# Layer-3 queries of batch 0 behind the last chunk's front, and a longer planned duration for ScalarE's sums

## The chip, the cores and the metric

One Trainium2 chip, one core. The metric is the device time of one execution in microseconds. An execution's profile gives its span, from the first to the last instruction.

## The reference

Two sequences of 1024 tokens with 256 features (`x`), and a context of 154 tokens for each, pass through four layers. Every layer adds a cross attention and then a feed-forward network, both on the layer-normed stream:

```python
x = x + xattn_0(layernorm(x), ctx);  x = x + ffn_0(layernorm(x))   # softmax attention; ternary weights, squared ReLU
x = x + xattn_1(layernorm(x), ctx);  x = x + ffn_1(layernorm(x))   # softmax attention; gathered experts + gated MLP
x = x + xattn_2(layernorm(x), ctx);  x = x + ffn_2(layernorm(x))   # attention with rotary positions; 8 experts, top 2, + shared
x = x + xattn_3(layernorm(x), ctx);  x = x + ffn_3(layernorm(x))   # autocorrelation; 8 experts, top 2
```

In layer 1 every token picks 32 of 4096 rows of a table (4 heads, top 8). It takes the product of its own state with each row's first half, and adds the rows' second halves weighted by silu(product) times a softmax weight. In layer 3 the attention is a correlation over time:

```python
corr = irfft(rfft(Q) * conj(rfft(K)));  w, idx = top_k(corr.mean(-1), 6);  w = softmax(w)
out = sum_k w_k * roll(V, -idx_k);  return out @ Wo + bo
```

## The kernel before

Tokens stand on the 128 partitions, 16 tiles of 128 tokens in all. The work goes by chunks of 512 tokens, 0 to 3; chunks 0 and 1 are batch 0, chunks 2 and 3 batch 1. The attentions of layers 0 to 2 run in the order `A_ORDER`, the last four being (2,0), (2,1), (2,2), (2,3), written as (layer, chunk). Behind each attention comes the FFN of the same layer and chunk, beside the next attention.

`plan()` describes all work as items with an engine, a duration, and the items that must come first. The durations stand in the table `DUR`, by engine and kind of item. A list scheduler then goes through time: at each step the engine that is free first takes, of the items that are due, the one with the longest path to the end (`rank`). So an item is never left waiting for a more urgent one that isn't due yet. The result is one fixed order for each engine. `build()` emits the instructions in that order, with semaphores for what one engine needs of another. On the chip an engine executes in its order, so it stalls where an item is later than planned.

The names that the change and the prediction touch:

- A front (`front`) is the layer norm of a chunk and its transposition. N1 on VectorE takes the statistics (L1434 to L1439), N2 on ScalarE the square root (L1199), N3 on VectorE the factors (L1445 to L1449), N4 on ScalarE normalises (L1210), X on TensorE transposes (L786) and X on ScalarE evicts (L1217). Fronts "a" belong to attention, "f" to an FFN, "q" to layer 3's queries, "z" to the layer-3 FFN. Items of one kind keep the order in which `plan()` adds them, on each engine.
- PSUM banks 4 and 5 are shared, in the order of the list `shared`, by fronts, queries, layer 3's keys (K3, L1046) and values (V3, L1057), and the down projections of the last layer-2 FFN (Y2).
- `queries3(c, space)` is a "q" front of chunk c, the query projection on TensorE (q3, L1067) and its eviction on ScalarE (L1336, L1338). The first correlation needs chunks 0 and 1, the second chunks 2 and 3.
- `ffn2`: logits (L1008), then ten gate-and-up steps (gu2: L1025 on TensorE, L1311 on ScalarE, L1664 on VectorE) and nine down projections (y2: L1037 on TensorE, L1673 or L1452 on VectorE).
- `correlate(b, ...)`: the correlation on TensorE (co, L1082, two halves), an eviction (L1346), a round trip through DRAM that shifts rows (`scr_corr`), a sum over features (tp, L1091), top six on VectorE, and a second round trip (`scr_roll`). Then `rolled` multiplies on TensorE (o3, L1103) and projects (y3, L1115), with the bias added on GpSimd (bo3, L1853).
- Spreads of keys and values for layer 3 on VectorE: ks3 (L1691) and vs3 (L1702). The values go through DRAM (`scr_v`) first.
- The layer-1 gather runs in 128 units of four rows for each partition, five units deep in a ring. GpSimd fetches (L1826), VectorE multiplies (mu, L1389), ScalarE sums each product in four activations and applies a tanh (`th`, L1184 and L1186), VectorE makes the weights (ew, L1396, L1397) and adds three rows (ad, L1406 to L1408), ScalarE weighs the fourth (L1193) and GpSimd adds it (L1840). After each tile VectorE adds GpSimd's part (ga, L1414). `ring_free` is the last of these.
- Attention: score maxima (p1: L829 on TensorE, L1516 on VectorE, eight of each), scores, exponentials (L1256), weighted values, and the out projection (L908 on TensorE, L1452 on VectorE).

SyncE issues the large loads and the round trips, in the planned order as well.

Of the kernel before, what the change touches and what calls it, by code (L numbers as in the profile page):

```python
# [55 lines left out]
def columns(pack):  # L56
    at, out = 0, {}
    for name, n in pack.items():
# [18 lines left out]
            gu1=4.9, y1=2.1, lg2=2.6, gu2=3.95, y2=2.4, K3=3.9, V3=6.4, q3=3.7, co=8.8, tp=3.0, o3=9.5, y3=2.0, lg3=2.2, gt3=0.6,  # L77
            be3=1.9, u3=1.9),
    ACT=dict(kv=0.9, N2=1.2, N4=2.05, X=1.1, Q=1.35, mt=0.6, s=2.4, r=1.4, w=0.6, o=0.6, h0=1.2, q1=1.15, gu1=1.45, 
             th=2.05, sc=0.5, lg2=1.4, gu2=1.1, K3=1.3, V3=1.2, q3=1.55, co=1.0, tp=0.5, o3=1.1, lg3=0.6, gt3=0.6),  # L80
    DVE=dict(kv=3.1, N1=2.05, N3=0.97, p1=1.45, t=0.64, y=0.43, h0=0.7, y0=0.43, sm1=3.9, gu1=0.69, mu=1.25,
             ew=0.41, ad=1.6, ga=0.42, Q=5.6, lg2=5.0, gu2=0.69, y2=1.5, ks3=2.95, vs3=2.9, tp=3.8, y3=0.85, l3=1.0, lg3=6.5,
             be3=1.9, u3=0.98),
# [9 lines left out]
def plan():  # L93
# [6 lines left out]
    def add(engine, item, dur, *first, land=0.0):  # L100
        dur = DUR[engine].get(item[0], dur) if engine in DUR else dur
        if (engine, item[0]) == ("PE", "y2") and item[2] == 8:
            dur *= 1.8
        first = [f if f[0] in todo else (f, SIGNAL) for f in first if f]
        if item[0] not in ("ld", "in"):
            if (engine, item[0]) in same:
                n = same[engine, item[0]]
                first.append((n, -todo[n][2]))
            same[engine, item[0]] = (engine, item)
        assert all(f in todo for f, _ in first), (item, first)  # L110
        todo[engine, item] = (dur, first, land)
        return engine, item
# [7 lines left out]
    def load(what, n, land, *first):  # L120
        ld[what, n] = add("SP", ("ld", what, n), 0.1, *first, land=land)

    def kv(layer, b):
        item = (layer, b)
        shared.append(("kv",) + item)
        old = (layer - 1, 2 * b + 1) if layer else None
        k1 = add("PE", ("kv",) + item, 3.6, ld["kv", layer], ("SP", ("in", "ctx")), ("SP", ("in", "const")), banks[0])
        k2 = add("ACT", ("kv",) + item, 0.9, k1, parts[0])
        k3 = add("DVE", ("kv",) + item, 7.5 if layer == 2 else 5.0, k2, old and ("PE", ("w",) + old + (G4 - 1,)),
                 ld["rope", 0 if b == 0 else 2] if layer == 2 else None)  # L130
        banks[0] = parts[0] = k3
        return k3

    def front(tgt, layer, c, *ready):
        item, f = (tgt, layer, c), len(fronts)
        fronts.append(item)
        shared.append(("X",) + item)
        n1 = add("DVE", ("N1",) + item, 2.7, small[f % 2], *ready)
        n2 = add("ACT", ("N2",) + item, 0.8, n1)
        n3 = add("DVE", ("N3",) + item, 1.3, n2)  # L140
        if (tgt, layer) == ("f", 1):
            free = ("DVE", ("mu", UNITS * (c - 1) - 1)) if c >= 2 else None
        else:
            free = use["xa"]
        n4 = add("ACT", ("N4",) + item, 2.4, n3, free, use["x1"])
        small[f % 2] = n4
        xt = "xta" if tgt in ("a", "q") or (tgt, c % 2) == ("z", 1) else "xtf"
        x1 = add("PE", ("X",) + item, 1.3, n4, banks[0], ("SP", ("in", "const")), use[xt])
        use["x1"] = x1
        if (tgt, layer) != ("f", 1):  # L150
            use["xa"] = x1
        x2 = add("ACT", ("X",) + item, 1.25, x1)
        banks[0] = x2
        return x2

    def queries(layer, c, xt, k):
        item = (layer, c)
        shared.append(("Q",) + item)
        q1 = add("PE", ("Q",) + item, 3.6, xt, ld["q", PIECE_AT[k]])
        use["xta"] = q1  # L160
        old = k >= 2 and ("PE", ("r",) + A_ORDER[k - 2] + (1,))
        if layer < 2:
            banks[0] = add("ACT", ("Q",) + item, 1.3, q1, old)
        else:
            banks[0] = add("DVE", ("Q",) + item, 5.0, q1, old, ld["rope", c])
        return banks[0]
# [125 lines left out]
    ring_free = ("DVE", ("ga", UNITS * NCH - 1))  # L292

    def kv3():
        shared.append(("K3",))
        p = add("PE", ("K3",), 5.2, ld["kv", 3], banks[0])
        k = banks[0] = add("ACT", ("K3",), 1.6, p, ring_free)
        shared.append(("V3",))
        p = add("PE", ("V3",), 5.2, ld["late", 0], banks[0])
        v = banks[0] = add("ACT", ("V3",), 1.4, p, ring_free)  # L300
        stored = add("SP", ("vw",), 0.4, v, land=2.2)
        return k, add("SP", ("vr",), 1.6, (stored, 0.0), land=4.0)

    def queries3(c, space):
        xt = front("q", 3, c, x_ready[3, c])
        shared.append(("Q3", c))
        p = add("PE", ("q3", c), 3.7, xt, ld["q", len(PIECES) - 1], banks[0])
        use["xta"] = p
        banks[0] = add("ACT", ("q3", c), 1.6, p, space)
        return banks[0]  # L310
# [20 lines left out]
    for k, (layer, c) in enumerate(A_ORDER):  # L331
        a_out = attention(layer, c, k, kv_in[layer, c // 2], q_in)
        if k in KV_AFTER:
            kl, kb = KV_AFTER[k]
            kv_in[kl, kb] = kv(kl, kb)
            if kb:
                load("kv", kl + 1, 5.0, kv_in[kl, kb])
        n = PIECE_AT[k]
        if k == RUNS[n][-1]:
            load("o", n + 1, 5.0, ("PE", ("y", layer, c, TI - 1)))  # L340
        if k + 1 < len(A_ORDER):
            nl, n_c = A_ORDER[k + 1]
            xt = front("a", nl, n_c, x_ready[nl, n_c])
            q_in = queries(nl, n_c, xt, k + 1)
            n = PIECE_AT[k + 1]
            if k + 1 == RUNS[n][-1]:
                load("q", n + 1, 5.0, q_in)
            if nl == 2 and n_c < NCH - 1:
                load("rope", n_c + 1, 6.0, ("DVE", ("Q", 2, n_c)))
        if k == len(A_ORDER) - 1:  # L350
            keys0, values_in = kv3()
            queries_in = [queries3(z, ring_free) for z in range(2)]
        xf = front("f", layer, c, a_out)
        if k == len(A_ORDER) - 1:
            queries_in.append(queries3(2, a_out))
        prev = (ffn0, ffn1, ffn2)[layer](c, xf, prev)
        x_ready[layer + 1, c] = ("DVE", ("ga", UNITS * (c + 1) - 1)) if layer == 1 else prev[0]
        if (layer, c) == (0, NCH - 1):
            load("rope", 0, 6.0, prev[0])
            load("f2a", 0, 12.0, prev[0])  # L360
        if (layer, c) == (1, NCH - 1):
            load("f2b", 0, 18.0, prev[0])
            load("late", 0, 15.0, ("DVE", ("ga", UNITS * NCH - 1)))
# [91 lines left out]

def build(nc, io):
    order, shared, fronts = plan()
    front_of = {item: f for f, item in enumerate(fronts)}

# [1621 lines left out]
```

## Time and profile before

| | us |
|---|---|
| median of 3 runs | 1735.56 |
| lowest and highest | 1729.33, 1751.61 |
| the profiled execution, its time | 1747.5 |
| its span | 1745.5 |
| its mean granted TensorE clock | 0.859 |

The profiled execution lies above the median by 11.9 us, within the spread of the runs. Busy time of an engine is the union of its instructions; for TensorE (PE) it says how long it worked, not how fast. A time in brackets behind a row of the timeline is the idle time of the engine just before, with what ended it.

### The profile page before, as it was taken

To read this page: it belongs to the slowest core of one execution; us is meant where nothing else is said; L and a number is where in the kernel's file an instruction comes from. 1 tells how busy PE (TensorE), PEld (TensorE's weight loads), DVE (VectorE), ACT (ScalarE), POOL (GpSimd) and SP (SyncE) were. 2 spreads that over 40 slices of the span, in tenths; PEclk is the share of its full clock that TensorE was granted. 3 is DMA by queue.
4 is the path that set the end of the run, shared out by engine and by line. 5 is a ranking of instruction groups with operands and counts; after the bars stand their busy time and mean duration, and the time that the engine had idled before them with its cause. 6 is when DMAs were issued, how large, how long until landed. Compare 5 with 4: busy or idle time off the path is not lost.

```text
span 1745.5 us, 18805 instructions
## 1 busy us (share of the span) xinstructions
PE 1320.8 (76%) x5858; PEld 661.1 (38%) x5858; DVE 1127.6 (65%) x2929; ACT 810.4 (46%) x2052; POOL 693.0 (40%) x705
## 2 busy tenths in 40 slices
PE   5889886747778586447667568677879978887998
PEld 3245443333344343213323333433444434533444
DVE  5542317579996777897898897996542433426365
ACT  2345442646658576438556649558234330210010
POOL 2000000468878777648868688884000010000000
PEclk8699898968899698668878789898889989997999
DMA  6000000455557556736546766663000121021000
GB/s 229 6 1 1 10 7 1 113 143 158 162 164 162 156 163 193 152 97 173 174 127 183 194 181 172 180 170 101 7 16 1 67 49 32 1 49 40 4 13 24
DMA packets 59380, 169.07 MB, mean 97 GB/s; under 512 B 15632, under 2 KB 20304, under 8 KB 58640
## 3 DMA queue, kind: packets, MB, share of 16 engines
q0 software_dynamic: 40960, 134.25, 28.9%
q1 hardware_dynamic: 18320, 33.61, 6.1%
q8 instruction: 47, 0.77, 0.2%
q14 instruction: 53, 0.43, 0.1%
HBM read 163.00 MB, written 4.82 MB: 96 GB/s over the span
## 4 chain that ended last, share of the span: by engine, by line
PE 40%; DVE 27%; ACT 13%; issue 9%; DMA 5%; POOL 3%; another core or an unknown queue 2%; SPq 1%; DVEq 0%; ACTq 0%; POOLq 0%
PE psum L1159 5%; PE psum L1025 4%; ACT bufR L1184 4%; DVE bufR L1389 3%; DVE bufB L1516 3%; POOL bufR L1826 3%; ACT bufR L1256 3%; PE psum L960 2%; PE psum L1103 2%; PE psum L952 2%; PE psum L1037 2%; DVE x_sb L1407 2%; PE psum L1082 2%; PE psum L829 2%
## 5 line engine op out<-in xcount | busy, mean ns | idle before, releaser
L1826 POOL DMA_INDIRECT bufR<-in_table,rowid x512 | 554.0, 1082 | 238.7 <-issue 127.5
L1184 ACT ACTIVATE bufR<-bufR 128x256 f32<-128x256 f32 x512 | 205.6, 405 | 85.1 <-DVE bufR L1389 69.7
L1389 DVE TENSOR_TENSOR bufR<-bufR 128x1024 f32<-128x1024 f32 x128 | 160.7, 1258 | 26.4 <-DMA bufR<-in_table,rowid 23.7
L829 PE MATMUL psum<-bufB 32*128 32x308 f32 x768 | 99.5, 596 | 101.4 <-DVE bufB L1516 76.3
L1025 PE MATMUL psum<-xtf,wf 128*128 128x512 f32 x320 | 153.5, 624 | 23.6 <-DVE x_sb L1452 11.5
L1516 DVE TENSOR_REDUCE bufB<-psum 128x8 f32<-128x1232 f32 x96 | 137.9, 1436 | 44.4 <-PE psum L829 42.9
L1853 POOL TENSOR_TENSOR x_sb<-x_sb,wattn 128x256 f32<-128x256 f32 x16 | 11.0, 723 | 310.0 <-DMA wattn<-in_attn 186.2
L1452 DVE TENSOR_TENSOR x_sb<-x_sb,psum 128x256 f32<-128x256 f32 x128 | 50.6, 417 | 118.3 <-PE psum L960 67.8
L1846 POOL TENSOR_TENSOR x_sb<-x_sb,wattn 128x256 f32<-128x256 f32 x32 | 23.5, 765 | 236.4 <-DMA wattn<-in_attn 158.3
L1786 DVE SCALAR_TENSOR_TENSOR x_sb<-psum,bufR,x_sb 128x256 f32<-128x256 f32 x128 | 61.9, 484 | 77.3 <-PE psum L1159 70.8
L1256 ACT ACTIVATE bufR<-psum 128x1024 f32<-128x1024 f32 x96 | 92.8, 1019 | 39.3 <-PE psum L855 37.3
L1193 ACT ACTIVATE bufR<-bufR,ew 128x256 f32<-128x256 f32 x128 | 64.0, 505 | 97.4 <-DVE ew L1397 64.5
L1840 POOL TENSOR_TENSOR half_sum<-half_sum,bufR 128x256 f32<-128x256 f32 x112 | 92.6, 827 | 34.4 <-ACT bufR L1193 32.2
L1037 PE MATMUL psum<-wf,bufR 128*128 128x256 f32 x320 | 89.0, 429 | 19.9 <-DVE bufR L1664 17.3
L1025 PEld LDWEIGHTS psum<-xtf,wf 128*128 128x128 f32 x320 | 60.8, 198 | 105.3 <-issue 71.2
L1184 ACT ACTIVATION_READ_ACCUMULATOR bufR<-bufR 128x1 f32 x512 | 97.0, 190 | 0.0
L829 PEld LDWEIGHTS psum<-bufB 32*128 32x128 f32 x768 | 37.4, 229 | 154.6 <-DVE bufB L1516 103.9
L853 PE MATMUL psum<-bufB 32*128 32x512 f32 x384 | 62.0, 717 | 35.9 <-ACT bufR L1256 23.3
L1037 PEld LDWEIGHTS psum<-wf,bufR 128*128 128x128 f32 x320 | 65.8, 214 | 49.2 <-issue 39.9
L991 PE MATMUL psum<-xtf,wf 128*128 128x512 f32 x128 | 73.4, 725 | 12.1 <-DVE bufR L1588 5.7
L1311 ACT ACTIVATE bufR<-psum 128x512 f32<-128x512 f32 x40 | 23.8, 594 | 123.5 <-PE psum L1025 123.5
L1673 DVE SCALAR_TENSOR_TENSOR x_sb<-psum,bufR,x_sb 128x256 f32<-128x256 f32 x128 | 53.0, 477 | 43.4 <-PE psum L1037 41.1
(236 smaller groups left out, 2582.0 us busy)
## 6 DMA issues: line engine op xcount, KB each, us to landing
bufR<-in_table,rowid POOLq DMA_INDIRECT x512
wf<-in_ffn SPq DMA_DIRECT2D x2, 2304.0 KB, 18.7
bufR<-in_ffn SPq DMA_DIRECT2D x1, 2696.5 KB, 16.9
wattn<-in_attn SPq DMA_DIRECT2D x4, 641.0 KB
wf<-in_rope SPq DMA_DIRECT2D x4, 512.0 KB
bufB<-in_ffn SPq DMA_DIRECT2D x1, 2048.0 KB, 8.5
scr_corr<-bufR SPq DMA_DIRECT2D x16, 128.0 KB, 2.4
bufR<-scr_corr SPq DMA_DIRECT2D x4, 512.0 KB
```

What stands on the lines that cost most here:

```text
L829: ins = mm(psum[:, z, 0:PAR * S], q[r, g, i * P:(i + 1) * P], keysm[r, g, b, :, 0:S], start=True, stop=True)
L991: ins = mm(bank(6 + r), w1(name)[:, kt, m * P:(m + 1) * P], xtf[:, kt, :], start=kt == 0, stop=kt == KT - 1)
L1025: ins = mm(bank(6 + r), gu[:, kt, r, :], xtf[:, kt, :], start=kt == 0, stop=kt == KT - 1)
L1037: ins = mm(psum[:, (4 if c == LAST else 6) + i // 2, i % 2 * D:(i % 2 + 1) * D], hm2[:, GUS.index(m) % 7, i * P:(i + 1) * P], down2[:, m, ...
L1159: ins = mm(bank(unit_bank3(c, y)), xt_of("z", c)[:, kt, i * P:(i + 1) * P], we3[:, kt, e * 512:(e + 1) * 512], start=kt == 0, stop=kt == K ...
L1184: own.mark(act(row, row, ACT.Identity, accum_out=dots[:, g % 4, j:j + 1]))
L1193: ins = act(row, row, ACT.Copy, scale=ew[:, g % 4, j:j + 1])
L1256: act(probs[side][:, par:4:2, :], psum[:, 2 * side:2 * side + 2, :], ACT.Exp).then_inc(at_ex, 1)
L1389: tt(rows, rows, cast(xg[c % 2][:, i, :].unsqueeze(1), [P, GRP, D]), ALU.mult).then_inc(f1_mu, 1)
L1516: eng.reduce_max(m4[:, i, :].rearrange("p (z r) -> p z r", z=BANDS)[:, :, PAR * g:PAR * g + PAR], psum[:, 0:BANDS, 0:PAR * S].rearrange("p ...
L1826: eng.indirect_dma_start(ring[:, s * GRP + j, :], None, io["table"], bass.IndirectOffsetOnAxis(ap=rowid[c % 2][:, at + j:at + j + 1], axis ...
L1840: eng.tensor_tensor(half_sum[:, :], half_sum[:, :], up, ALU.add).then_inc(f1_half, 1)
```

## The change

Layer 3's queries of chunks 0 and 1 are added to the plan after the front "f" of chunk 3 of layer 2, and no longer before it. So on each engine their fronts come after that front, their transposes and projections use the shared banks after its transposes, and the first correlation, which needs them, comes after all of this. The queries of chunk 2 follow as before. The keys and values of layer 3 stay ahead of the front. The second edit sets the planned duration of `th` on ScalarE from 2.05 to 2.75. It changes no instruction, only the orders that the scheduler finds.

```diff
-             th=2.05, sc=0.5, lg2=1.4, ...
+             th=2.75, sc=0.5, lg2=1.4, ...
@@
         if k == len(A_ORDER) - 1:
             keys0, values_in = kv3()
-            queries_in = [queries3(z, ring_free) for z in range(2)]
         xf = front("f", layer, c, a_out)
         if k == len(A_ORDER) - 1:
-            queries_in.append(queries3(2, a_out))
+            queries_in = [queries3(z, a_out if z == 2 else ring_free) for z in range(3)]
         prev = (ffn0, ffn1, ffn2)[layer](c, xf, prev)
```

## Rows read from the trace of the kernel before

**Rows 1.** The page: busy time, share of the span; the chain that ended last.
```profile
PE 1320.8 (76%) x5858; PEld 661.1 (38%) x5858; DVE 1127.6 (65%) x2929; ACT 810.4 (46%) x2052; POOL 693.0 (40%) x705
...
PE 40%; DVE 27%; ACT 13%; issue 9%; DMA 5%; POOL 3%; another core or an unknown queue 2%; SPq 1%; DVEq 0%; ACTq 0%; POOLq 0%
```
**Rows 2.** Timeline (start us, us, engine, line, operation): last gathered tile, chunk 3's first maxima.
```profile
1209.37 0.43 DVE L1414 TENSOR_TENSOR x_sb<-x_sb,half_sum 128x256 f32<-128x256 f32 x1 [0.95 <-POOL half_sum L1840]
...
1255.24 0.80 PE L829 MATMUL psum<-bufB 32*128 32x308 f32 x8
```
**Rows 3.** Windows: stretch, length, busy PE, PEld, DVE, ACT, POOL, granted clock, DMA.
```profile
1255.00:1387.00 132.00, 112.09 (x474) 58.84 (x473) 52.87 (x143) 49.99 (x76) 0.00 (x0) 0.91 0.04 8
1386.94:1411.95 25.01, 25.00 (x201) 10.86 (x200) 14.28 (x54) 11.08 (x19) 5.51 (x8) 1.00 0.45 148
1411.95:1421.80 9.85, 0.00 (x0) 0.00 (x1) 0.69 (x1) 0.60 (x1) 0.00 (x0) 0.74 0.39 106
1421.80:1463.73 41.93, 36.12 (x96) 17.53 (x96) 25.27 (x44) 7.59 (x12) 0.00 (x0) 0.94 0.14 33
1463.73:1513.85 50.12, 50.12 (x296) 25.53 (x296) 13.65 (x31) 5.84 (x9) 0.00 (x0) 0.97 0.00 1
```
**Rows 4.** Timeline of TensorE, 1261 to 1324.
```profile
1261.69 1.94 PE L786 MATMUL psum<-const,xa 128*128 128x128 f32 x8 [2.33 <-ACT xa L1210]
...
1295.50 3.70 PE L1067 MATMUL psum<-xta,wattn 128*128 128x512 f32 x8
1309.37 6.09 PE L1025 MATMUL psum<-xtf,wf 128*128 128x512 f32 x8 [10.17 <-DVE x_sb L1452]
...
1315.73 1.04 PE L786 MATMUL psum<-const,xa 128*128 128x128 f32 x8
...
1319.85 3.60 PE L1067 MATMUL psum<-xta,wattn 128*128 128x512 f32 x8
```
**Rows 5.** Timeline of VectorE, the spread of layer 3's values.
```profile
1305.10 2.89 DVE L1702 TENSOR_TENSOR bufR<-bufR,const 128x1280 f32<-128x1280 f32 x2 [12.33 <-DMA bufR<-scr_v]
```
**Rows 6.** Timeline of TensorE, 1385 to 1406.
```profile
1385.05 1.97 PE L1037 MATMUL psum<-wf,bufR 128*128 128x256 f32 x8 [0.34 <-DVE bufR L1664]
1386.94 8.81 PE L1082 MATMUL psum<-bufR 64*64 64x512 f32 x80
1395.69 1.09 PE L786 MATMUL psum<-const,xa 128*128 128x128 f32 x8
1396.71 8.81 PE L1082 MATMUL psum<-bufR 64*64 64x512 f32 x80
```
**Rows 7.** Timeline of VectorE, between statistics and factors of chunk 3's front.
```profile
1388.78 2.88 DVE L1691 TENSOR_TENSOR bufB<-bufR,const 128x1280 f32<-128x1280 f32 x2
```
**Rows 8.** Timeline of ScalarE, 1392 to 1400.
```profile
1392.63 2.08 ACT L1210 ACTIVATE xa<-x_sb,shift,rstd 128x256 f32<-128x256 f32 x4 [5.10 <-DVE shift L1449]
...
1396.81 1.08 ACT L1217 ACTIVATE xtf<-psum 128x512 f32<-128x512 f32 x2
1397.76 2.07 ACT L1210 ACTIVATE xa<-x_sb,shift,rstd 128x256 f32<-128x256 f32 x4
```
**Rows 9.** Timeline of ScalarE, last piece of the first query block's eviction.
```profile
1300.73 0.40 ACT L1338 ACTIVATE bufR<-psum,wattn 128x160 f32<-128x160 f32 x1
```
**Rows 10.** Timeline of TensorE, behind the two round trips of batch 0.
```profile
1421.80 6.12 PE L1091 MATMUL psum<-bufR,const 128*32 128x512 f32 x8 [9.86 <-DMA bufR<-scr_corr]
...
1463.73 10.51 PE L1103 MATMUL psum<-bufR 64*64 64x512 f32 x80 [4.69 <-DMA bufR<-scr_roll]
```
**Rows 11.** Groups of ScalarE, 320 to 1215: busy us, mean ns, idle before.
```profile
L1184 ACT ACTIVATE bufR<-bufR 128x256 f32<-128x256 f32 x512 | 205.6, 405 | 85.1 <-DVE bufR L1389 69.7 <-issue 14.2
...
L1186 ACT ACT_TABLE_LOAD x13 | 16.7, 1283 | 0.2
```
**Rows 12.** Waits of VectorE and of GpSimd, whole span: us in total, times, longest.
```profile
DVE ew L1396 <- ACT thalf L1186: 23.3, 23, 3.8
...
POOL half_sum L1840 <- ACT bufR L1193: 32.2, 10, 7.6
```

More of the change, by code:

```diff
@@ L79 @@
     ACT=dict(kv=0.9, N2=1.2, N4=2.05, X=1.1, Q=1.35, mt=0.6, s=2.4, r=1.4, w=0.6, o=0.6, h0=1.2, q1=1.15, gu1=1.45,
-             th=2.05, sc=0.5, lg2=1.4, gu2=1.1, K3=1.3, V3=1.2, q3=1.55, co=1.0, tp=0.5, o3=1.1, lg3=0.6, gt3=0.6),
+             th=2.75, sc=0.5, lg2=1.4, gu2=1.1, K3=1.3, V3=1.2, q3=1.55, co=1.0, tp=0.5, o3=1.1, lg3=0.6, gt3=0.6),
     DVE=dict(kv=3.1, N1=2.05, N3=0.97, p1=1.45, t=0.64, y=0.43, h0=0.7, y0=0.43, sm1=3.9, gu1=0.69, mu=1.25,
```

## The prediction

> **What bounds the kernel now.** I read the page first. TensorE is busy 76% of the span, VectorE 65%, and the chain that ended last lies 40% on TensorE, 27% on VectorE and 13% on ScalarE [rows 1]. Only 3% of it lies on GpSimd, although GpSimd is busy 693 us, nearly all of it with the gather. The last gathered tile is added at 1209.37, and the attention of the last chunk, which waits for it, starts only at 1255.24 [rows 2]. So the gather has slack, and what decides is the order in which TensorE, VectorE and ScalarE walk through attention and FFN.
>
> The change touches two places by name. From 1255 to 1387 the attention of chunk 3 runs beside the layer-2 FFN of chunk 2, with TensorE busy 112.1 of 132 us. From 1386.94 on, the first correlation of layer 3 runs and hides its own round trips to DRAM behind the FFN of chunk 3. Up to 1513.85 TensorE is busy 25.0, 0, 36.1 and 50.1 us in the four stretches, together 111.2 of 126.9 us [rows 3]. The moved block costs what TensorE has no idle time for.
>
> **The moved queries, in their old place.** Each of the two blocks is 8 transposes and 8 matmuls: 1.04 + 3.60 us for the second, and the first has the same work with 3.70 us in its matmuls, together 9.4 us of TensorE [rows 4]. The first pair lies just before a TensorE gap of 10.17 us that ends at 1309.37. Its cause is on VectorE, which stood 12.33 us before L1702, the spread values of layer 3, until their DMA had landed [rows 5]. That landing counts from the values' eviction, which the queries don't touch, so taking the first pair away only makes this gap longer: gain 0. The second pair lies in a busy stretch, with the scores of chunk 3 waiting behind its 3.60 us of L1067. Bounds of the gain: 0 and the pair's 4.6 us. I take 4.0, nearer the pair's own size, since TensorE idles only 20 of the 132 us of this stretch and half of that in the one gap. **Term 1: -4.0.**
>
> **The front with nothing to cover it.** Before, the first correlation starts at 1386.94, the moment the last down projection ends, and runs 8.81 us. The transposes of the front of chunk 3 come after it without a gap, at 1395.69 [rows 6]. After, the correlation needs queries that now stand behind this front. The front itself runs late: between its statistics and its scale factors VectorE spends 2.88 us, until 1391.66, on L1691, a spread of layer 3's keys [rows 7]; ScalarE normalises from 1392.63 to 1394.71 [rows 8]. TensorE has ended its last layer-2 product of chunk 2 at 1387.02 and has nothing else that is ready, so it idles 1394.71 - 1387.02 = 7.7 us. The least is 7.7 - 2.88 = 4.8, if L1691 falls elsewhere; the most is 7.7 plus the 3.70 us of one FFN step, if the planner has run that step earlier and thus widened the hole. **Term 2: +7.7.**
>
> **Half clock behind the gap.** The granted clock is 1.00, the upper level of 2.4 GHz, from 1386.94 to 1411.95, where TensorE never idles, and 0.74 in the mean over the gap that follows [rows 3]. The same eight transposes take 1.94 us after a wait and 1.04 us in a busy stretch, and the FFN step behind the 10.17 us gap took 6.09 instead of 3.70 us [rows 4]. So such a gap costs 0.9 to 2.4 us more. **Term 3: +2**, nearer the upper end, because that row stands behind a gap of like length.
> This is also the place where a rule speaks against the change. The Trainium skill (TensorE: Matmul & The Clock Gate, Part 1) says the array drops to half rate when it has idled and returns to full rate only after it has been busy again. By the rule everything right behind the gap would run at 1.2 GHz, as the FFN step of 6.09 us did, so the term would be 2.4 and the sum below 12.0; by the transposes' row alone it would be 0.9 and the sum 10.5.
>
> **The moved work in its new place.** The 9.4 us come back between the front and the correlation. The path there, from rows: transposes end 1396.78, the next normalisation ends 1399.83 (3.1 us), transposes 1.1, eviction 1.1 [rows 6, 8], matmuls 3.6, their eviction 1.9 (matmuls ended 1299.20, last piece out at 1301.13) [rows 4, 9], again transposes 1.1 and eviction 1.1, matmuls 3.6, eviction 1.3 (the second block has no short piece): 17.9 us. FFN steps of 3.7 us of chunk 3 fit into the holes and can't be interrupted, so I let each of three steps delay it by some 1.7 us, about half its length, and the path grows to 23 us while TensorE stays busy. Idle left in it: 0 to 3 us, I take 1.5. **Term 4: +9.4, term 5: +1.5.** The correlation starts 7.7 + 1.1 + 23 = 32 us later than before, less term 1.
>
> **Does the later chain cost those 32 us?** No. Its round trips keep their length: 16.3 us from 1405.5 to 1421.80, of which TensorE idled 9.86, and 35.8 us from 1427.9 to 1463.73, of which it idled 4.69 [rows 6, 10]. But behind 1463.73, TensorE was busy 50.1 of 50.1 us [rows 3], a good part of it with FFN steps of chunk 3. Three such steps (11 us) and the logits now run ahead of the correlation, so about 12 us leave that last stretch. By the chain the loss is 32 - 12 - 4 = 16 us, by terms 1 to 5 it is 16.6. The two agree; I take 16.6. The bias of layer 3 on GpSimd waits for the second query front. It takes 5.5 us [rows 3] and is needed only behind both round trips, 52 us later; without that cover it would cost its 5.5 us. SyncE issues the same DMAs in the same order, so its queue costs nothing.
>
> **ScalarE's planned duration.** No instruction changes; only the planner's order. Between 320 and 1215 us each of the 128 units has four activations of 405 ns, 1.6 us, and little more around them; 13 of the units also load a table, for 1283 ns [rows 11]. So 2.05 fits the usual unit, and 2.75 lies between it and one with a table. The effect: work that waits for the sums is put later in VectorE's order. What it can give back is VectorE's waits for the tanh, 23.3 us in 23 places [rows 12]. What it can cost is later releases of ring slots: GpSimd already waits 32.2 us for ScalarE [rows 12], though with slack behind it [rows 2]. Bounds: -23.3 and, for orders turned the wrong way, +10 (one stall like that of 10.17 us). I take **term 6: -5**, since each single wait is small, 1 us in the mean, and the order is shuffled everywhere.
>
> **Sum:** -4.0 + 7.7 + 2 + 9.4 + 1.5 - 5 = **+11.6 us**. It is made on the profiled execution (1745.5 span, 1747.5 its time), 0.7% above the median of 1735.6; the difference carries over: 1735.6 + 11.6 = **1747 us**.
>
> **Rivals.**
> A, faster or level: the 12.33 us wait of VectorE moves off the path. The planner reckons the values back some 10 us after their matmuls; with one block of transposes less on TensorE, the last maxima of chunk 3 come due within about 1 us of that. If they are put ahead of L1702, the gap of 10.17 us and its half clock of 2.4 us vanish: 11.6 - 12.6 = -1, so 1735. For it: the near tie. Against: the planner never leaves an engine idle that has something due, and by its numbers the values are due first.
> B, faster: the longer duration takes away all 23.3 us of waits instead of 5: 11.6 - 18.3 = -7, so 1729. Against: they are 23 waits of 1.0 us in the mean among 128 units, so most units meet none now.
> C, slower: the FFN steps don't go ahead of the correlation, so the 12 us are not given back and the round trips run dry: 32 - 4 - 5 = +23, so 1759. It decides if fewer than two steps stand between the front and the correlation. With an unlucky reorder of +10 instead of -5 it is 1774.
> D: the reorder in layers 1 and 2 alone turns out bad by 10: 11.6 + 15 = +27, so 1762. For it: attention there shares VectorE with the gather's sums, and a wait set too early stalls both.
>
> **Chances.** Forecast 0.50 (its own range 1738 to 1755), A 0.12, B 0.13, C 0.15, D 0.10. The range from 1722 (A and B in part together) to 1768 (C or D with a little more) leaves out 2 in 10. Beyond 2%, 35 us, which is about what a measurement of this kernel can tell: faster 0.05, slower 0.10, within 0.85.
>
> **What would show it.** Right: an idle TensorE of 5 to 11 us right after the attention of chunk 3, the transposes of its front with about 1.9 us, the first correlation some 28 us later relative to it, the wait before L1702 still 10 us or more, TensorE's wait for the correlation's DMA still 8 to 10 us. The attention of chunk 3 starts within 10 us of 1255. Wrong: that start has moved by more than 10 us (then term 6 is mis-sized), or the span from the end of this attention to the end is longer by less than 10 or more than 30 us (terms 2 to 5).

## The result and the profile after

The changed kernel takes 1770.2 us (median of 4 runs, 1767.7 to 1773.2), the kernel before, run beside it, 1732.4 (median of 4, 1727.1 to 1751.6). The ratio is 1.0198, 95% interval 1.0116 to 1.028: about 34 us slower. The interval lies on both sides of 2%, so whether the change costs more than that is not settled. Predicted were 11.6 us and a range up to 1768, so the direction held and the size did not: 1770.2 lies just above the range.

The profiled execution of after spans 1765.7 us, that of before 1745.5. The unchanged kernel was profiled a second time (run e10) and spans 1721.0. So the profile of before on which the prediction rests was a long one, and a stage of after is compared with both profiles of before.

The page of after, busy time and chain that ended last:

```profile
PE 1342.5 (76%) x5858; PEld 670.8 (38%) x5858; DVE 1123.5 (64%) x2929; ACT 816.9 (46%) x2055; POOL 689.6 (39%) x705
...
PE 37%; DVE 22%; POOL 18%; issue 11%; DMA 5%; ACT 5%; SPq 1%; another core or an unknown queue 0%; DVEq 0%; POOLq 0%; ACTq 0%
```

GpSimd's share of the chain is 18%, where it was 3% in [rows 1]. TensorE is busy 22 us longer with the same 5858 matmuls, the other engines as long as before within 7 us. The mean granted clock of the profiled executions is 0.848 after and 0.859 and 0.857 in the two of before; how much of the 34 us is matmuls that ran slower was not separated. The same line of the second profile of before:

```profile
PE 38%; DVE 23%; POOL 13%; issue 9%; ACT 9%; DMA 5%; SPq 1%; another core or an unknown queue 1%; DVEq 0%; POOLq 0%; ACTq 0%
```

So GpSimd, and with it the gather, lay on the path of the unchanged kernel too, in one execution of two. The chain of one execution is one way back; that of another execution of the same kernel differs.

Last gathered tile and first maxima of chunk 3, as in [rows 2], first after, then the second profile of before:

```profile
1204.14 0.43 DVE L1413 TENSOR_TENSOR x_sb<-x_sb,half_sum 128x256 f32<-128x256 f32 x1
...
1256.97 0.80 PE L828 MATMUL psum<-bufB 32*128 32x308 f32 x8 [1.22 <-DVE x_sb L1451]
```
```profile
1193.32 0.42 DVE L1414 TENSOR_TENSOR x_sb<-x_sb,half_sum 128x256 f32<-128x256 f32 x1 [0.96 <-POOL half_sum L1840]
...
1237.10 0.80 PE L829 MATMUL psum<-bufB 32*128 32x308 f32 x8
```

From the end of the gather to the attention of chunk 3 there are 45.4 us in [rows 2], 43.4 us in the second profile, and 52.4 us after. The gather ended 16 us apart in the two profiles of before and the attention of chunk 3 started 18 us apart, so the two move together. That doesn't show that the one waits for the other. By its seventh tile the gather was already 14 us apart (740.2 and 726.2), and the attention of chunk 2 started 15 us apart (1119.7 and 1104.8). Between the end of the gather and chunk 3's maxima TensorE is busy 41 of 45 us and 40 of 43. The last tile itself is not what chunk 3 waits for. In the first profile its front is evicted at 1221.53, and the projection that reads it runs 8.9 us later, without a wait of TensorE:

```profile
1220.45 1.08 ACT L1217 ACTIVATE xta<-psum 128x512 f32<-128x512 f32 x2
...
1230.42 3.60 PE L796 MATMUL psum<-xta,wattn 128*128 128x512 f32 x8
```

In the second profile the same distance is 8.9 us as well.

TensorE of after, from the end of chunk 3's attention to the first correlation (compare [rows 6]):

```profile
1376.61 1.97 PE L1036 MATMUL psum<-wf,bufR 128*128 128x256 f32 x8 [0.34 <-DVE bufR L1663]
1380.47 3.70 PE L1024 MATMUL psum<-xtf,wf 128*128 128x512 f32 x8 [1.89 <-DVE x_sb L1672]
1385.53 1.07 PE L785 MATMUL psum<-const,xa 128*128 128x128 f32 x8 [1.36 <-ACT xa L1209]
1389.59 3.75 PE L1036 MATMUL psum<-wf,bufR 128*128 128x256 f32 x8 [3.00 <-DVE bufR L1663]
1393.13 1.91 PE L785 MATMUL psum<-const,xa 128*128 128x128 f32 x8
...
1400.68 3.60 PE L1024 MATMUL psum<-xtf,wf 128*128 128x512 f32 x8
...
1405.76 3.70 PE L1024 MATMUL psum<-xtf,wf 128*128 128x512 f32 x8 [0.61 <-DVE bufR L1663]
...
1412.73 3.60 PE L1024 MATMUL psum<-xtf,wf 128*128 128x512 f32 x8
1416.26 17.40 PE L1081 MATMUL psum<-bufR 64*64 64x512 f32 x160
```

The front idles 1.89 + 1.36 + 3.00 = 6.25 us, the query chain 0.61, and three gate-and-up steps of chunk 3 (L1024) run between front and correlation. The correlation starts 32.1 us after the end (1384.17) of the last such step of chunk 2, where it started 4.0 us after it in the second profile of before. Counted from the end of chunk 3's attention, the correlation starts after 40.0 us, and after 2.2 in both profiles of before.

TensorE of after, behind the round trips of batch 0 (compare [rows 10]):

```profile
1450.17 5.34 PE L1090 MATMUL psum<-bufR,const 128*32 128x512 f32 x8 [10.57 <-DMA bufR<-scr_corr]
...
1465.69 3.70 PE L1024 MATMUL psum<-xtf,wf 128*128 128x512 f32 x8 [1.37 <-DVE bufR L1663]
...
1474.11 5.40 PE L1024 MATMUL psum<-xtf,wf 128*128 128x512 f32 x8 [2.71 <-DVE bufR L1663]
...
1491.05 10.57 PE L1102 MATMUL psum<-bufR 64*64 64x512 f32 x80 [6.39 <-DMA bufR<-scr_roll]
```

The waits are 10.57 and 6.39 us instead of 9.86 and 4.69 (9.28 and 2.61 in the second profile of before), and new ones stand between them.

### The profile page after: what moved, and what is told of

The parts are those of the page before. It is cut to its first block, busy times and chain, and to the rows that moved or that the text cites. A ratio compares the mean times of both kernels' runs of the same rounds, so it can differ in the third digit from the quotient of the medians.

```text
span 1765.7 us, 18808 instructions
## 1 busy us (share of the span) xinstructions
PE 1342.5 (76%) x5858; PEld 670.8 (38%) x5858; DVE 1123.5 (64%) x2929; ACT 816.9 (46%) x2055; POOL 689.6 (39%) x705
## 3 DMA queue, kind: packets, MB, share of 16 engines
q0 software_dynamic: 40960, 134.25, 27.5%
## 4 chain that ended last, share of the span: by engine, by line
PE 37%; DVE 22%; POOL 18%; issue 11%; DMA 5%; ACT 5%; SPq 1%; another core or an unknown queue 0%; DVEq 0%; POOLq 0%; ACTq 0%
POOL bufR L1825 15%; PE psum L1158 5%; PE psum L1024 4%; DVE bufB L1515 3%; POOL half_sum L1839 2%; PE psum L1102 2%; PE psum L1081 2%; DVE bufR L1388 2%; PE psum L1036 2%; PE psum L828 2%; PE psum L959 2%; PE psum L852 2%; PE psum L877 2%; ACT bufR L1255 2%; PE psum L795 1%
## 5 line engine op out<-in xcount | busy, mean ns | idle before, releaser
L1024 PE MATMUL psum<-xtf,wf 128*128 128x512 f32 x320 | 163.0, 656 | 37.0 <-DVE x_sb L1672 15.4
L1845 POOL TENSOR_TENSOR x_sb<-x_sb,wattn 128x256 f32<-128x256 f32 x32 | 24.5, 797 | 234.2 <-DMA wattn<-in_attn 157.8
L1024 PEld LDWEIGHTS psum<-xtf,wf 128*128 128x128 f32 x320 | 64.2, 210 | 124.4 <-issue 75.1
L1839 POOL TENSOR_TENSOR half_sum<-half_sum,bufR 128x256 f32<-128x256 f32 x112 | 91.3, 815 | 41.1 <-ACT bufR L1192 38.9
L1036 PE MATMUL psum<-wf,bufR 128*128 128x256 f32 x320 | 85.0, 415 | 17.6 <-DVE bufR L1663 14.0
L828 PEld LDWEIGHTS psum<-bufB 32*128 32x128 f32 x768 | 38.2, 234 | 141.6 <-DVE bufB L1515 86.0
L990 PE MATMUL psum<-xtf,wf 128*128 128x512 f32 x128 | 73.4, 726 | 12.0 <-DVE bufR L1587 8.3
L1406 DVE SCALAR_TENSOR_TENSOR x_sb<-bufR,ew,x_sb 128x256 f32<-128x256 f32 x128 | 71.0, 555 | 4.5
```

Of the source, the lines that this page charges most:

```text
L828: ins = mm(psum[:, z, 0:PAR * S], q[r, g, i * P:(i + 1) * P], keysm[r, g, b, :, 0:S], start=True, stop=True)
L990: ins = mm(bank(6 + r), w1(name)[:, kt, m * P:(m + 1) * P], xtf[:, kt, :], start=kt == 0, stop=kt == KT - 1)
L1024: ins = mm(bank(6 + r), gu[:, kt, r, :], xtf[:, kt, :], start=kt == 0, stop=kt == KT - 1)
L1036: ins = mm(psum[:, (4 if c == LAST else 6) + i // 2, i % 2 * D:(i % 2 + 1) * D], hm2[:, GUS.index(m) % 7, i * P:(i + 1) * P], down2[:, m, ...
L1839: eng.tensor_tensor(half_sum[:, :], half_sum[:, :], up, ALU.add).then_inc(f1_half, 1)
```

## The experiments

Lines named in the runs with the move are one lower than before, for everything behind `plan()`.

**e1, the move alone; e2, the duration alone.** The diffs are the second and the first hunk of the change.

> The queries of chunks 0 and 1 behind the front, the planned duration of the sums left at 2.05. The planned orders of all engines are then those of the kernel before up to the last chunk's attention. Theory 1 (the move costs by the uncovered front and the moved work, and the longer duration costs on its own upstream): the time from the first maxima of chunk 3 to the end of the span grows by 18 us, from 490.3 to about 508.7 as in the changed kernel; that start stays where the kernel before has it (within its own spread); median 1.010 to 1.013 of the kernel before, about 1752. Rival (the move makes the whole difference, the duration nothing): 1.020, about 1768.

> The planned duration of the sums at 2.75, the queries left ahead of the front. Theory 1: from the first maxima of chunk 3 to the end 490 us as before; that start is later than in a usual execution of the kernel before by some 15 to 20 us, so 1.009 to 1.012, about 1750. Rival (the duration costs nothing): 1.000 within 0.4%. My forecast of a gain of 5 us would show as 0.997.

Measured: e1 1751.9 (6 runs), ratio 1.0122 (1.0074 to 1.0171); e2 1745.4 (12 runs), ratio 1.0083 (1.0049 to 1.0118). The product, 1.0206, is close to the whole change's 1.0198. So the move costs 21 us (13 to 30), near the 16.6 of terms 1 to 5, and the planned duration costs 14 us (8 to 20), where a gain of 5 was predicted.

**e10, the kernel before, profiled once more.** No edit.

> The kernel before, unchanged, profiled once more to see where an execution near the median spends less than the first profile. Theory: the span is 10 to 20 us below 1745.5; the part from the first maxima of chunk 3 to the end takes 484 to 487 us instead of 490.2, and the rest is lost in the gather stretch; the time from the first maxima of chunk 2 to those of chunk 3 is 133 to 136 us, as in every execution with this order so far. Rival: that stretch varies by 10 us or more by itself, so that the 148 us with the longer planned duration say nothing.

Span 1721.0, 24.5 us below the first profile, more than the 10 to 20 expected. From the first maxima of chunk 3 to the end it takes 483.9 us, and from those of chunk 2 to those of chunk 3 132.3. Against it e1 can be read stage by stage. Windows from the first maxima of chunk 3 to the end of the last gate-and-up step of chunk 2, and from the first correlation to the end of batch 0's output projection; the columns are those of [rows 3]. The second profile of before, then e1:

```profile
1237.10:1364.70 127.60, 107.94 (x454) 56.01 (x454) 49.56 (x131) 48.13 (x74) 0.00 (x0) 0.91 0.03 6
1368.70:1491.10 122.40, 109.39 (x586) 52.51 (x586) 52.04 (x124) 25.11 (x41) 5.51 (x8) 0.94 0.17 50
```
```profile
1239.70:1364.50 124.80, 100.01 (x429) 51.07 (x428) 50.69 (x129) 41.33 (x59) 0.00 (x0) 0.90 0.09 27
1395.90:1515.90 120.00, 98.23 (x538) 45.98 (x537) 39.30 (x71) 15.86 (x24) 0.00 (x0) 0.91 0.12 29
```

First stretch: 7.9 us less work on TensorE, 2.8 us shorter. Between the stretches: 4.0 us became 31.4. Second stretch: TensorE's work fell by 11.2 us, the length by 2.4 only, and the idle time rose from 13.0 to 21.8. Behind it 230.0 and 231.6 us are left. Together -2.8 + 27.4 - 2.4 + 1.6 = 23.8 us, beside 21 by the ratio. Against the first profile of before the same four are -3.0, +27.5, -5.0 and -2.0, together 17.5. So what is given back behind the correlation is between 1 and 7 us, by the profile that is taken.

**e14, the move with the round trips planned at about their real length.** Can the cost of the move be a matter of what stands in the round trips?

```diff
-        turned = add("SP", ("cr", b), 0.2, (stored, 0.0), values, land=3.5)
+        turned = add("SP", ("cr", b), 0.2, (stored, 0.0), values, land=9.5)
...
-        return add("SP", ("rr", b), 0.2, (stored, 0.0), land=4.5)
+        return add("SP", ("rr", b), 0.2, (stored, 0.0), land=12.5)
```

> The move alone, with the landings of the two round trips of layer 3 planned at 9.5 and 12.5 us, near what the traces show, instead of 3.5 and 4.5. Theory (half of the moved delay isn't given back because TensorE idles in the round trips of batch 0, 22 us against 16 in the kernel before, with FFN steps planned behind the waits): the sum over features comes behind one FFN step and one projection, TensorE's wait before it falls from 10.6 to under 4 us, the stretch from the last half of the correlation to the end of the layer-3 projection shortens by 4 to 8 us, ratio 1.007 to 1.010. Rival (the round trips are the path and TensorE's idle time costs nothing): the ratio stays at 1.012.

1731.9 (12 runs) beside 1731.95 of before: ratio 0.9974 (0.9944 to 1.0005), where e1 had 1.0122. That is a larger gain than the 1.007 to 1.010 expected. The same two places of TensorE's timeline in e14:

```profile
1450.25 3.62 PE L1090 MATMUL psum<-bufR,const 128*32 128x512 f32 x8 [1.76 <-DMA bufR<-scr_corr]
...
1491.44 8.81 PE L1102 MATMUL psum<-bufR 64*64 64x512 f32 x80
```

The wait for `scr_corr` is 1.76 us and that for `scr_roll` is gone. The front still idles (1.90 + 2.86 + 1.98 us by its rows) and the correlation still starts late, 42.4 us behind the attention of chunk 3 (40.0 after, 2.2 before). The stretch from the correlation to the end of batch 0's output projection is what became short:

```profile
1415.90:1517.60 101.70, 92.82 (x537) 45.48 (x536) 39.22 (x71) 15.87 (x24) 0.00 (x0) 0.98 0.15 35
```

101.7 us with 8.9 idle, where e1 had 120.0 with 21.8. So the path could shorten once more steps stood in the round trips. Of the 18.3 us that the stretch lost, 12.9 are idle time and 5.4 are TensorE's work, which is the same matmuls at a mean granted clock of 0.98 instead of 0.91. The new landing times hold for batch 1's round trips as well: behind this stretch 221.4 us are left, 10 less than in e1. So not all of the gain is the filling of batch 0's trips. In e1 the scheduler believed that the data would land 6 and 8 us earlier than e14 plans, took the urgent item to be due, put it next in TensorE's list, and TensorE stood behind it with other work ready.

**e8 and e15, half of the move.** Queries of chunk 0 ahead of the front, of chunk 1 behind it; e15 is the same kernel again.

```diff
-            queries_in = [queries3(z, ring_free) for z in range(2)]
+            queries_in = [queries3(0, ring_free)]
...
-            queries_in.append(queries3(2, a_out))
+            queries_in += [queries3(z, a_out if z == 2 else ring_free) for z in (1, 2)]
```

> Only chunk 1's queries behind the front; chunk 0's stay ahead of it. Theory (uncovered front 5 to 8 us, plus 4.6 us of moved work, less up to 4 us gained in the old place): the first correlation starts 18 to 21 us later relative to the end of the attention instead of 37 to 40 in the changed kernel, and the ratio is 1.004 to 1.008. Rival (the cost is the moved work alone, in proportion): half of the full move, about 1.005, but with no idle TensorE in front of the transposes. Rival (the cost is the uncovered front alone): the same ratio as the full move, 1.010.

> The half move once more, since its trace (10 us more than the kernel before from the first maxima of chunk 3 to the end) and its median (18 us more) differ. If the trace is right: ratio 1.005 to 1.007; if the median is: 1.009 to 1.011.

e8: 1746.9 (12 runs), ratio 1.0102 (1.0072 to 1.0132). e15: 1750.8 (6 runs), ratio 1.0124 (1.0075 to 1.0173). Half the move costs about as much as the whole; e8 lies above the 1.004 to 1.008 of its forecast, at the 1.010 of the rival that the uncovered front alone costs, and e15, above both of its own forecasts, confirms it. By stages both profiles lose some 12 us: from the first maxima of chunk 3 to the end of batch 0's output projection they take 265.6 and 266.1 us, the second profile of before 253.9. The correlation starts 24.4 us after the attention instead of 2.2, and the round trips again leave TensorE dry (7.88 and 7.41 us before L1103). The rest of the 18 to 21 us appears at no one place: behind that projection e8 has 228.0 us and e15 236.3. That part is open, and with it whether that rival is right.

**e5 and e13, the values of layer 3 planned later.** These are the kernel before with another landing time, 14 in e5 and 20 in e13. They test whether the VectorE wait of [rows 5] makes TensorE's gap of [rows 4].

```diff
-        return k, add("SP", ("vr",), 1.6, (stored, 0.0), land=4.0)
+        return k, add("SP", ("vr",), 1.6, (stored, 0.0), land=20)
```

> The kernel before with one planned number changed: the landing of layer 3's values is planned 14 us instead of 4 us after the last issue, which moves the spread of the values behind the last maxima and the down projection of the shared experts on VectorE, and changes no other order. Theory (the 10 us gap of TensorE is on the path): the 12.3 us wait of VectorE shrinks below 6 us, the attention of chunk 3 ends 8 to 12 us sooner after its start, ratio 0.993 to 0.995. Rival (the stretch is bound by the FFN's own steps or the wait reappears one item later): within 3 us, 0.998 to 1.000.

> The kernel before with the landing of layer 3's values planned 20 us instead of 4, so that their spread also stands behind the first routed FFN step on VectorE. Theory (TensorE's gap is wholly made by this wait): no TensorE gap over 4 us between 1285 and 1320, the gain grows from 7 us to 10 to 14 us, ratio 0.992 to 0.994. Rival (what remains is the FFN's own chain of steps): 0.995 to 0.997 as with 14.

e5: 1722.3 (12 runs), 0.9959 (0.9931 to 0.9987). e13: 1716.0 (12 runs), 0.9933 (0.9903 to 0.9963). VectorE before L1702 in e5, then in e13:

```profile
1301.03 2.89 DVE L1702 TENSOR_TENSOR bufR<-bufR,const 128x1280 f32<-128x1280 f32 x2 [7.56 <-DMA bufR<-scr_v]
```
```profile
1296.03 2.89 DVE L1702 TENSOR_TENSOR bufR<-bufR,const 128x1280 f32<-128x1280 f32 x2 [1.13 <-DMA bufR<-scr_v]
```

The wait falls from 12.33 to 7.56 and 1.13 us, and the gap of TensorE from 10.17 to 3.57 and nothing. The wait in e5 stayed above the 6 us expected and its gain just below the forecast; e13 came out as forecast. The time falls by 7.1 and 11.6 us of 1727.9. The gap with its half clock had been priced at 12.6 in rival A.

**e17, after with the values planned later.** The same edit (20) in the changed kernel.

> The changed kernel with the values planned 20 us late. Theory (the gap of 11.9 us that the wait for the values makes in TensorE is on the path after the change as before it): ratio against the kernel before falls from 1.020 to 1.012 to 1.015. Rival (with the queries gone, attention has slack there and only the FFN of chunk 2 gains): 1.017 to 1.020.

1756.1 (6 runs), 1.0135 (1.0095 to 1.0175). Divided by after's 1.0198 that is 0.994, the gain of e13. So the VectorE wait had not gone anywhere in after. Its rows there, VectorE and then TensorE:

```profile
1294.34 1.44 DVE L1515 TENSOR_REDUCE bufB<-psum 128x8 f32<-128x1232 f32 x1 [0.40 <-PE psum L828]
1308.12 2.90 DVE L1701 TENSOR_TENSOR bufR<-bufR,const 128x1280 f32<-128x1280 f32 x2 [12.35 <-DMA bufR<-scr_v]
```
```profile
1300.06 0.42 PE L854 MATMUL psum<-bufB 32*128 32x512 bf16 x4
1312.39 6.04 PE L1024 MATMUL psum<-xtf,wf 128*128 128x512 f32 x8 [11.91 <-DVE x_sb L1451]
```

The last maxima did come ahead of the wait, as rival A said. But TensorE then had only one piece of scores more to do and stood 11.91 us, behind the next thing that VectorE owed.

**e16, the kernel before with all three landing times corrected** (20, 9.5 and 12.5, no move).

> The kernel before with the values planned 20 us, the round trips 9.5 and 12.5 us late. Theory: the gain of the values stays (12 us), and the first correlation goes ahead of the last layer-2 FFN step of chunk 2, so it starts 4 to 6 us sooner: ratio 0.989 to 0.992. Rival (the step put behind it is then missed by the next front): no better than 0.993.

1712.1 (12 runs), ratio 0.990 (0.9871 to 0.9928): faster than both kernels. TensorE waits 3.82 us for `scr_corr` and not at all for `scr_roll`. Against e13's 0.9933 the two round trips bring 0.3%, some 6 us, which is not clear of the noise, where they brought 25 us with the move (1.0122 to 0.9974). The edit of e14 without the move and without e13's was not run; by e16 over e13 it would be about 0.9967 (an estimate), beside e14's 0.9974. So with these landing times the move would cost about nothing, give or take the 3 parts in 1000 of each ratio.

**e11 and e12, where the longer duration does its harm.** The order of one planning run up to the first maxima of chunk 2, that of the other behind them. e11 is planned with 2.05 first and 2.75 behind, e12 the other way round.

```diff
-def plan():
+def plan_one(moved, th):
...
+        dur = th if (engine, item[0]) == ("ACT", "th") else dur
...
+def plan():
+    head, _, _, start = plan_one(*(False, 2.05))
+    tail, shared, fronts, _ = plan_one(*(False, 2.75))
+    cut = start["PE", ("p1", 2, 2, 0)]
+    early = {n for n, t in start.items() if t < cut}
+    order = {e: [i for i in head[e] if (e, i) in early] + [i for i in tail[e] if (e, i) not in early] for e in head}
```

> Queries as in the kernel before. All items that the old plan starts ahead of the first maxima of chunk 2 in layer 2 stand in the order planned with 2.05, all later ones in the order planned with 2.75. Theory (the longer duration costs through the order of VectorE around the maxima of chunk 2, where 38 instead of 32 items stand between the first and the last maximum): these maxima take 63 to 66 us instead of 50 to 55, chunk 3's start 146 to 150 us after chunk 2's, ratio 1.006 to 1.010. Rival (the loss comes from orders further up, which only show there): ratio within 0.3% of 1.

> The mirror image: the order planned with 2.75 up to the first maxima of chunk 2, the order planned with 2.05 behind. Theory: maxima of chunk 2 within 50 to 57 us, chunk 3's start 133 to 137 us after chunk 2's, ratio 0.997 to 1.003. Rival (loss further up): 1.006 to 1.010.

e11: 1738.1 (12 runs), 1.008 (1.0049 to 1.011). e12: 1735.8 (12 runs), 1.0067 (1.0038 to 1.0096); its expectation of 0.997 to 1.003 missed, that of e11 held for the ratio. Each half of the new order costs nearly as much as the whole (1.0083). The sum of the two, 1.0147, lies outside the interval of the whole, though not by much beside their own intervals. Why they don't add up is not shown.

In the early half GpSimd waits longer. Its timeline in e2:

```profile
733.75 0.75 POOL L1840 TENSOR_TENSOR half_sum<-half_sum,bufR 128x256 f32<-128x256 f32 x1
754.60 0.73 POOL L1840 TENSOR_TENSOR half_sum<-half_sum,bufR 128x256 f32<-128x256 f32 x1 [20.11 <-ACT bufR L1193]
767.41 1.70 POOL L1826 DMA_INDIRECT bufR<-in_table,rowid  x1 [12.08 <-DVE prob L1623]
```

No such pair stands in the second profile of before, where the longest waits there are 8.92 and 2.36 us. Over the whole span, GpSimd's waits within the gather (for ScalarE's fourth row, the new row numbers, and VectorE's third row) in the second profile of before, then in e2:

```profile
POOL bufR L1826 <- DVE prob L1623: 72.9, 1, 72.9
POOL half_sum L1840 <- ACT bufR L1193: 29.2, 12, 7.6
POOL bufR L1826 <- DVE x_sb L1408: 22.4, 10, 8.9
```
```profile
POOL bufR L1826 <- DVE prob L1623: 85.4, 2, 73.3
POOL half_sum L1840 <- ACT bufR L1193: 44.1, 9, 20.1
POOL bufR L1826 <- DVE x_sb L1408: 10.3, 6, 2.7
```

The sums are 124.5 and 139.8. In all profiles whose early half was planned with 2.05 (ten of them) the sum is 117 to 137, mean 129.6; in the four planned with 2.75 (after, e2, e12, e17) 139.5 to 142.6, mean 141.0. So GpSimd waits 11 us more within the gather. These 11 us don't arrive at its end. With 2.75 the seventh tile is done at 718 us in the mean of the four profiles, with 2.05 at 731; the eighth, with the waits above, at 794 in both; the last at 1205.5 and 1200.7. That end varies by 20 us from one execution to the next, so the 4.8 us between the means are not clear of it. Where the early half costs is seen below, on VectorE.

Both halves leave their trace in one place, the score maxima of chunk 2, which VectorE takes from what TensorE has multiplied. These are windows from TensorE's first matmul for them to the end of VectorE's last maximum, first the first profile of before, then e2; VectorE's busy time stands third:

```profile
1119.70:1171.00 51.30, 32.48 (x142) 17.34 (x142) 47.30 (x108) 29.35 (x103) 42.28 (x43) 0.83 0.65 171
```
```profile
1106.00:1173.00 67.00, 44.47 (x164) 25.01 (x165) 62.16 (x137) 35.86 (x126) 55.03 (x56) 0.80 0.62 172
```

VectorE is busy 92% and 93% of them, so it has next to no room there. The table has means and ranges over all 14 profiles. The first row sorts them by the number that the early half was planned with, the other two by that of the late half:

| | planned with 2.05 (ten profiles) | with 2.75 (four) |
|---|---|---|
| TensorE's first matmul to VectorE's first maximum | 10.4 us (9.0 to 12.1) | 17.4 (16.4 to 18.2) |
| VectorE's first maximum to its last | 41.1 (38.2 to 43.4) | 46.5 (45.3 to 48.3) |
| from there to the first maxima of chunk 3 | 83.8 (81.0 to 86.4) | 84.7 (82.4 to 87.5) |

The early order brings VectorE to this attention with more of its list undone: it runs 28 to 31 instructions before its first maximum instead of 17 to 19, and comes 7.0 us later. The late order has 39 items on VectorE from the first to the last maximum instead of 33 (one more unit of the gather, the sum of a tile, a gate-and-up step and a down projection), and these take 5.4 us more. e11 and e12 each show one and not the other: 12.1 and 48.3 us in e11, 16.4 and 41.1 in e12. What follows is equally long. The expectations were less exact: in e11 the maxima took less than the 63 to 66 us forecast, and in e12 chunk 3's maxima started 141 us after chunk 2's instead of 133 to 137.

## Why the prediction was off

| step | predicted | measured |
|---|---|---|
| term 1, queries gone from the old place | -4.0 | -2.8 (e1 over e10) |
| the correlation later, by the chain | +32 | +27.4 |
| given back behind the correlation | -12 | -2.4, then +1.6 (-5.0 and -2.0 over the first profile) |
| the move in all | +16 by the chain, +16.6 by terms | +21 (13 to 30) |
| term 6, planned duration | -5 | +14 (8 to 20) |
| sum | +11.6 | +34 |

**Term 1** holds. The first stretch lost 7.9 us of TensorE's work and only 2.8 us of its length, which fits the reading that the pair ahead of the gap is worth nothing.

**Terms 2 to 5** hold nearly, counted from the last gate-and-up step of chunk 2. The sign in the prediction, "some 28 us later relative to" the end of the attention, came out as 37.8: without the queries the attention ran ahead, and the last steps of chunk 2's FFN now stand behind it. The front idles 6.25 us, predicted 7.7, within the stated 5 to 11. The prediction had L1691 in it; VectorE now runs that spread behind the front's factors, and the idle time comes in three pieces around a gate-and-up step and a down projection of chunk 2, waiting twice for VectorE and once for ScalarE. "The front transposes take about 1.9 us" did not come true; they take 1.07, and the next ones, those of the first query block, take 1.91. The windows of after around these, the columns as before, show the clock:

```profile
1384.20:1393.10 8.90, 4.58 (x16) 3.61 (x17) 5.86 (x22) 7.49 (x13) 0.00 (x0) 0.76 0.07 25
1393.10:1397.20 4.10, 4.01 (x26) 3.60 (x24) 3.61 (x13) 2.71 (x6) 0.00 (x0) 0.69 0.02 4
1397.20:1416.30 19.10, 18.49 (x53) 8.36 (x53) 7.83 (x30) 10.55 (x19) 5.49 (x8) 1.00 0.00 0
```

The mean granted clock is 0.76 and 0.69 over 13 us, a mixture of its two levels, and 1.00 behind. So the half clock came a little later than in the text. It cost 1.8 us in the down projection at 1389.59 (3.75 us, where the same work took 1.97 at 1376.61) and 0.9 in the transposes at 1393.13, together 2.7, near the 2 taken. Behind the long idle of 11.91 us a step took 6.04 us, as in [rows 4]. The Trainium skill (TensorE: Matmul & The Clock Gate, Part 1) says that an array that has idled runs at half rate until it has been busy again. The 6.04 us agree with it; right behind the short idles of 1.89 and 1.36 us the steps ran at full rate (3.70 and 1.07 us), behind that of 2.71 us at 1474.11 a step of 3.70 us took 5.40.

**The step that failed in the move** is "about 12 us leave that last stretch". Its first half was right: 11.2 us of TensorE's work did leave the stretch behind the correlation, and three gate-and-up steps did run ahead of it. Its second half took work that leaves for time that leaves. The stretch holds two round trips that keep their length (16.5 and 35.5 us in after, 16.3 and 35.8 in the prediction's rows), and the steps that left were the ones that covered them. The stretch became 2.4 us shorter instead of 12 (5.0 over the first profile), and its idle time grew by 8.8. Rival C named the mechanism ("the round trips run dry") but tied it to the wrong condition, that the steps don't go ahead of the correlation. They did, and that is why the trips ran dry. e14 shows how much hangs on this term: with later planned landings, and so more work in the trips, the whole cost of the move disappears, though part of that gain lies in batch 1's trips.

**Term 6** had the wrong sign, which is the larger error, 19 of the 22 us. What the prediction wanted to gain was gained: VectorE's waits for the tanh fell from 23.3 us in 23 places to

```profile
DVE ew L1395 <- ACT thalf L1185: 11.2, 9, 2.0
...
POOL half_sum L1839 <- ACT bufR L1192: 38.9, 7, 17.0
```

in after (17.2 in 16 places in the second profile of before). It didn't shorten the time. The step that failed is the sign of the reorder: the prediction counted the waits that it takes away, and bounded its harm by later releases of ring slots, which it then set aside with "the gather has slack". Two things rested on that. First, the chain with 3% of GpSimd: it has 13% in the second profile and 18% in after, and GpSimd's waits grew, though the gather's end moved less than they did. Second, the list of VectorE, which the prediction didn't look at: by the table above the reorder brings VectorE to chunk 2's attention 7 us late and puts six more items between its maxima, 5 us more, in a stretch where VectorE is busy 92%. Rival D had this reason ("attention there shares VectorE with the gather's sums") and nearly this size (bad by 10), with a chance of 0.10. "The gather has slack" was half right: its last tile has some 9 us by the rows above, but its units share VectorE and ScalarE with the attention of chunk 2, and there they cost.

**The check that deceived.** "The attention of chunk 3 starts within 10 us of 1255" held, at 1256.97, and would have cleared term 6. But the 1255.24 of before was itself a late one: the second profile has 1237.10, and the nine profiles with both halves planned with 2.05 lie between 1233 and 1255, mean 1245; after, e2 and e17 between 1254 and 1259, mean 1256. The 11 us between the means are most of the 14; they arise in the maxima of chunk 2, which TensorE starts at 1107 us in the mean of after, e2 and e17 and at 1110 in the nine. The other sign of being wrong, the span from the end of chunk 3's attention to the end longer by more than 30 us, gave no clear answer either: 389.4 us in after are 28.6 more than in the first profile and 34.9 more than in the second. The spans of the two profiles of before differ by 24.5 us, more than any term of the sum.

What stays open: why half the move costs as much as the whole, and why the halves of the new order cost 8.0 and 6.7 parts in 1000 each and only 8.3 together, where the stages add up (7.0 and 5.4 us). Executions with one order differ by up to 20 us in the end of the gather (1189.6 to 1209.8).

## What to carry to other kernels

When a plan moves work ahead of a stretch with DMA round trips, ask what will cover the trips then; the work that leaves is worth only what the stretch's idle time doesn't grow by. In a kernel whose order comes from a planner, compare its landing times with the trace before anything else: three corrected numbers gave 1% here, and two of them decided whether another edit cost anything. Call nothing slack from one profile, and no dependence from a distance that stays the same: both ends may follow something earlier. Before a longer planned duration is given to an item, look at what the new order puts in front of and between the items of an attention, on the engine that is full there.

## What the runs showed of the hardware

- The unchanged kernel ran from 1712.9 to 1751.6 us over all four groups of runs, and from 1712.9 to 1737.4 within one of them (29 runs), with the same instructions in the same order. Of the 24.5 us between the two profiled executions, 16 are there by the end of the gather and 14 of them by its seventh tile. What makes them is not shown.
- The idle time just before a step doesn't by itself tell its rate: a gate-and-up step took 3.70 us behind 1.89 and 1.37 us of idle TensorE, and 5.40 behind 2.71 (after) and behind 1.90 (e14).
- The values of layer 3 come back from DRAM in 32 transfers of 10 KB, each with a median of 1.7 us to landing by the page of after. With a planned landing of 20 us the spread still waits 1.13 us, with 14 it waits 7.56, with 4 it waits 12.33. Whether the number of transfers makes this was not tried.
